# A new layout in SBUF for the split adjacency slices of a one-core GNN + LSTM kernel

## What is computed

```python
h = item_feat @ W_item.T + b_item            # 10000 x 128
b = layernorm(x) @ W_user.T + b_user
x = x + relu(adj @ h + b)                    # adj: 10000 x 10000, float32
xn = layernorm(x)[None]
hs = lstm(xn, W_ih, W_hh, b_ih, b_hh)
g  = argmax(hs @ W_lin.T + b_lin)            # gates what the two sums add up
w  = g * hs
x  = x + (2 * hs + (cumsum(w) - w) * fw_att + (total(w) - cumsum(w)) * bw_att)
```

## The kernel before

| slice, chunk | L882 (hi, item_hi) | L883 (lo, item_hi) | L884 (hi, item_lo) |
|---|---|---|---|
| 0, first | 64 | 192 | 256 |
| 0, second | 16 | 144 | 208 |
| 1, first | 480 | 96 | 160 |
| 1, second | 432 | 48 | 112 |
| 2, first | 384 | 0 | 64 |
| 2, second | 336 | 464 | 16 |
| 3, first | 288 | 416 | 480 |
| 3, second | 240 | 368 | 432 |

## Time and profile before

### The profile page before, as it was taken

How to read it: one execution, slowest core, us unless ns; L and a number is a source line. 1 busy time by engine, 2 the same in 40 slices (tenths; PEclk the granted TensorE clock), 3 DMA queues, 4 the chain that set the end, 5 groups by cost and what they waited for, 6 DMA issues and landing times.

```text
span 1427.8 us, 26195 instructions
## 1 busy us (share of the span) xinstructions
PE 1401.8 (98%) x7438; PEld 1210.5 (85%) x7438; DVE 1273.0 (89%) x2102; ACT 1056.4 (74%) x1449; POOL 213.4 (15%) x189
## 2 busy tenths in 40 slices
PE   8999999999999999999999999999999999999995
PEld 7888888888888888888888888888888899999995
DVE  7999999999999999999999999999999766676667
ACT  5677787777877877877877877877877676556663
POOL 0000000001001001001001001001000132036776
PEclk9999999999999999999999999999999999999998
DMA  9999999999999999999999999999999303000003
GB/s 373 344 336 382 399 387 392 394 385 383 405 385 395 391 387 397 392 382 402 384 387 402 391 377 405 387 380 402 388 388 382 133 1 144 0 2 0 0 0 145
DMA packets 143466, 442.96 MB, mean 310 GB/s; under 512 B 23944, under 2 KB 43337, under 8 KB 143307
## 3 DMA queue, kind: packets, MB, share of 16 engines
q1 hardware_dynamic: 126048, 426.43, 76.7%
q10 hardware_dynamic: 17387, 16.14, 4.0%
HBM read 432.15 MB, written 10.36 MB: 310 GB/s over the span
## 4 chain that ended last, share of the span: by engine, by line
PE 93%; DVE 5%; ACT 0%; issue 0%; DMA 0%; POOL 0%; ACTq 0%; DVEq 0%
PE psG L882 24%; PE psG L883 24%; PE psG L884 24%; PE psZ L980 10%; PE psZ L966 3%; PE psZ L968 3%; PE psZ L970 3%; DVE a_lo L1201 2%; PE psZ L986 1%; PE psT L857 1%; PE psI L930 1%; DVE item_lo L1234 1%; DVE u L1516 1%; DVE u L1215 0%; PE psG L875 0%
## 5 line engine op out<-in xcount | busy, mean ns | idle before, releaser
L665 ACT ACTIVATE a_hi<-raw 128x1000 fp32r<-128x1000 f32 (+1 forms) x800 | 819.5, 1030 | 241.9 <-PE psG L884 212.7
L1201 DVE TENSOR_TENSOR a_lo<-raw,a_hi 128x1000 fp32r<-128x1000 f32 (+1 forms) x800 | 897.8, 1171 | 22.9 <-ACT a_hi L665 19.9
L882 PE MATMUL psG<-a_hi,item_hi 128*128 128x500 f32 x1560 | 611.3, 392 | 2.3 <-DVE a_lo L1201 1.4
L883 PE MATMUL psG<-a_lo,item_hi 128*128 128x500 f32 x1560 | 606.0, 388 | 0.0
L884 PE MATMUL psG<-a_hi,item_lo 128*128 128x500 f32 x1560 | 604.6, 388 | 0.0
L882 PEld LDWEIGHTS psG<-a_hi,item_hi 128*128 128x128 f32 x1560 | 293.5, 188 | 65.5 <-DVE a_lo L1201 3.5
L884 PEld LDWEIGHTS psG<-a_hi,item_lo 128*128 128x128 f32 x1560 | 293.1, 188 | 59.5
L883 PEld LDWEIGHTS psG<-a_lo,item_hi 128*128 128x128 f32 x1560 | 293.7, 188 | 55.5
L980 PE MATMUL psZ<-hist,wh 128*128 (+1 forms) x1264 | 167.1, 275 | 2.9 <-DVE hist L1354 2.2
L980 PEld LDWEIGHTS psZ<-hist,wh 128*128 128x128 f32 x1264 | 154.0, 191 | 3.8 <-issue 2.4
L466 POOL TENSOR_TENSOR row_terms<-var,minus_half 125x4 f32<-125x4 f32 x20 | 37.6, 1878 | 677.9 <-DVE var L1152 677.9
(11 more groups left out here) (186 smaller groups left out, 857.1 us busy)
## 6 DMA issues: line engine op xcount, KB each, us to landing
raw<-in_adj_main SPq DMA_DIRECT2D x760, 500.0 KB, 6.6
raw<-in_adj_main SPq DMA_DIRECT2D x40, 250.0 KB, 4.7
sq<-rstd_copy ACTq DMA_DIRECT2D x20, 250.0 KB, 7.0
u<-x_copy SPq DMA_DIRECT2D x1, 5000.0 KB, 14.4
x_copy<-x_rows SPq DMA_DIRECT2D x19, 250.0 KB, 7.2
sq<-rows_copy ACTq DMA_DIRECT2D x19, 250.0 KB, 5.3
un_bb<-rows_copy ACTq DMA_DIRECT2D x19, 250.0 KB, 7.6
u<-in_itemT SPq DMA_DIRECT2D x9, 512.0 KB, 8.0
```

The source lines that it names most:

```text
L665: nc.scalar.activation(a_hi[:, s % CUT, 0:n], raw[:, r % RAW, at:at + n], ACT.Copy)\
L882: pe.matmul(bank, w_hi, hi, start=(c == 0), stop=False)
L883: pe.matmul(bank, w_hi, lo, start=False, stop=False)
L1201: last = dve.tensor_tensor(a_lo[:, s % CUT, 0:m], raw[:, r % RAW, at:at + m], a_hi[:, s % CUT, 0:m].bitcast(f32), ALU.subtract)
```

## The change

The two tensors `a_hi` and `a_lo` become one, `a_both`, in which places are worked out by numbers. The two chunks of a half piece begin 2048 bytes apart (`CHUNK = 512` elements) and not 2000, the slices 4048 bytes apart (`SLOT = 1012`) and not 4000. `item_tail` and `inv_rows` lose their own tensors and lie in columns of `x1_rows` that are not used yet at that time.

```diff
+CHUNK, SLOT = 512, 1012
+HI_AT, LO_AT, BOTH = 44, 4140, 8200
-        inv_rows = sb("inv_rows", [2, P])
-        item_tail = sb("item_tail", [P, STACKED], f32, first)
-        a_hi = sb("a_hi", [P, CUT, HALF * BW], f32r, first)
-        a_lo = sb("a_lo", [P, CUT, HALF * BW], f32r, first)
+        a_both = sb("a_both", [P, BOTH], f32r, first)
+        item_tail = x1_rows[:, 2 * HID:2 * HID + STACKED]
+        inv_rows = x1_rows[0:2, 3 * HID:4 * HID]
+        def chunk(at, s, i):
+            a = at + s % CUT * SLOT + i * CHUNK
+            return a_both[:, a:a + BW]
+        def chunks(at, s, n=HALF):
+            if n == 1:
+                return chunk(at, s, 0)
+            a = at + s % CUT * SLOT
+            return a_both[:, a:a + n * CHUNK].rearrange("p (c k) -> p c k", k=CHUNK)[:, :, 0:BW]
+        def by_chunk(t, n):
+            return t.rearrange("p (c k) -> p c k", k=BW) if n > BW else t
...
-                nc.scalar.activation(a_hi[:, s % CUT, 0:n], raw[:, r % RAW, at:at + n], ACT.Copy)\
+                nc.scalar.activation(chunks(HI_AT, s, n // BW), by_chunk(raw[:, r % RAW, at:at + n], n), ACT.Copy)\
...
-                            hi = a_hi[:, s % CUT, i * BW:(i + 1) * BW]
-                            lo = a_lo[:, s % CUT, i * BW:(i + 1) * BW]
+                            hi = chunk(HI_AT, s, i)
+                            lo = chunk(LO_AT, s, i)
...
-                last = dve.tensor_tensor(a_lo[:, s % CUT, 0:m], raw[:, r % RAW, at:at + m],
-                                         a_hi[:, s % CUT, 0:m].bitcast(f32), ALU.subtract)
+                last = dve.tensor_tensor(chunks(LO_AT, s, m // BW), by_chunk(raw[:, r % RAW, at:at + m], m),
+                                         chunks(HI_AT, s, m // BW).bitcast(f32), ALU.subtract)
```

More of the change, by code:

```diff
@@ L875, in body @@
                                 last = pe.matmul(bank, item_hi[0:STACKED, c * HID:(c + 1) * HID],
-                                                 a_hi[0:STACKED, s % CUT, i * BW:(i + 1) * BW], start=False, stop=True)
+                                                 chunk(HI_AT, s, i)[0:STACKED], start=False, stop=True)
                                 continue
-                            hi = a_hi[:, s % CUT, i * BW:(i + 1) * BW]
-                            lo = a_lo[:, s % CUT, i * BW:(i + 1) * BW]
+                            hi = chunk(HI_AT, s, i)
+                            lo = chunk(LO_AT, s, i)
                             w_hi = item_hi[:, c * HID:(c + 1) * HID]
@@ L1200, in split_lo @@
                 m = n - BW if tail else n
-                last = dve.tensor_tensor(a_lo[:, s % CUT, 0:m], raw[:, r % RAW, at:at + m],
-                                         a_hi[:, s % CUT, 0:m].bitcast(f32), ALU.subtract)
+                last = dve.tensor_tensor(chunks(LO_AT, s, m // BW), by_chunk(raw[:, r % RAW, at:at + m], m),
+                                         chunks(HI_AT, s, m // BW).bitcast(f32), ALU.subtract)
                 if tail:
                     mid = slice(STACK[1], STACK[1] + TAIL)
-                    last = dve.tensor_tensor(a_hi[mid, s % CUT, m:n], raw[mid, r % RAW, at + m:at + n],
-                                             a_hi[mid, s % CUT, m:n].bitcast(f32), ALU.subtract)
+                    short = chunk(HI_AT, s, 1)[mid]
+                    last = dve.tensor_tensor(short, raw[mid, r % RAW, at + m:at + n], short.bitcast(f32),
+                                             ALU.subtract)
                 last.then_inc(lo_ready, 1)
```

## The result

The changed kernel takes 1432.26 us (median of 11 executions), and the kernel before, on the same chips, 1427.95 us. The ratio is 1.0024, with a 95% interval of 1.0016 to 1.0033: 0.24% or 3.4 us slower (the two medians by themselves are 4.3 us apart). The forecast was 1425 us, 0.3% faster, with slower as a rival. The time is inside the range, the sign is wrong.

The account below looks back on a forecast made before the run. TensorE's matmul rate was taken as the bound. The four offsets' prices, 0.95 ns less on each of 4680 matmuls, gave -4.5 us from 1429.6, all other parts 0: 1425 us, range 1408 to 1439.

Parts of the forecast that it names:

- What bounds the kernel: TensorE, busy 98% of the span, sets the time of the 20 blocks; VectorE stands 2.6 us a block behind.
- Two runs of 500, `item_tail` and `inv_rows`, the LSTM at 0: Split ScalarE and VectorE accesses, moved first-block tensors, and the 303 us LSTM: each was to add 0 us.
- I price an offset with a matmul of before that has it to its own weights: TensorE's products: offsets 432, 384, 336, 288 priced at 383, 388, 389, 387 ns, mean 386.75; -4.5 us in all.
- The mean of before, taken as 387.7: Mean recorded duration of TensorE's 4680 matmuls before the change, 387.7 ns, against which the new offsets' 386.75 was set.
- The premise that a product lasts the same each time round the ring: TensorE's matmuls: the same slice and chunk gives the same duration each turn, with few exceptions; equal matmuls differ by 11 ns.
- 336 with 393 and 385 ns: One TensorE product at offset 336: 393 ns in the steady turn, 385 after a short stall; priced at the middle, 389.
- Rival B: One common offset lets TensorE's reads settle, most products near 383 ns: -22 us, 1408 us; chance 0.20.
- Rival C: Operand addresses modulo 512 do not cause TensorE's differing durations, so nothing changes: 1429.6 us; chance 0.15.
- Rival D: The weights loaded while a product streams matter: mean 390.75 ns, +14 us, 1444 us, half of that 1437; chance 0.25.

Follow-up runs that it names:

- the undo run: The changed kernel with slices back at the old offsets and `item_tail` its own tensor again, `a_both` and moved `inv_rows` kept: 1428.76 us, ratio 1.0003.
- the rings: TensorE alone playing the kernels' slice layouts, 144 distances each: before 225.6, changed 226.7, 16 bytes further 225.3, all slices at 448 220.0 ns.
- the map: TensorE alone, only matmuls, a run of 45 for each offset from 0 to 496, one start: 448 settled on 220.0 ns, 432 on 226.6.
- the pairs of the first map: TensorE alone, two weight tiles in turn at two distances to one moving chunk: 220.0 ns with both at 192 modulo 256; with 192 and 64, 220.0 or 228.

## Why the prediction was wrong

- **What bounds the kernel: right.** TensorE's distance from start to start set the time of both kernels (at 220 ns VectorE began to hold it back in places), and 0.9 ns on 4680 matmuls, 4.2 us, stands beside a measured 3.4 us by the ratio and 4.3 us by the medians.
- **Two runs of 500, `item_tail` and `inv_rows`, the LSTM at 0: right as far as shown.** VectorE's instruction took 1169 ns against 1171, and from the start of the last product to the end of the span there are 302.3 us in both profiles. With `inv_rows` moved the undo run had the time of before. `item_tail` was not tried alone, and TensorE reads both in the first block, which the prediction passes over; the rings leave no time for a cost of theirs. The price of the two runs was also less well founded than it reads: the runs of L1215 in the earlier trace rows lie without gaps.
- **"I price an offset with a matmul of before that has it to its own weights": this step failed.** It priced 432 at 383, 384 at 388, 336 at 389, 288 at 387 ns. Measured over blocks 2 to 20 they are 389.9, 388.8, 388.5 and 388.1, and the mean is 388.8 in place of 386.75. Of these 2.05 ns, 1.7 come from 432 alone. The mean of before, taken as 387.7, was right. The two products from which it was priced do stay short in the kernel before (382.7 and 383.8 ns in the mean), but in another sequence of offsets; in a run by itself on TensorE alone, and with all slices at 432, the offset gives 226.7 ns from start to start. The premise that a product lasts the same each time round the ring was also too strong: it holds within 1 ns for some nine in ten of the products of slices 1 to 3, and for six in ten of slice 0's first chunk. The row that could have warned me was in my own sum: 336 with 393 and 385 ns, for one product and one place. I took the middle of the two instead of asking what a value that depends on its predecessors says of a kernel with other predecessors.
- **Rival B, that a common offset helps:** the mechanism exists, since a run with one offset settles. But at half of the offsets in the map it settles on 226.7 ns, and at others on more or less. And the change keeps an offset for six products only, and none of its four (432, 384, 336, 288) stands at 220.0 in the map.
- **Rival C, that addresses are not the cause:** refuted, by the 18.7 us between 432 and 448. The Trainium skill, "SBUF — State Buffer", section "Who interferes with whom", says that TensorE's two read ports are independent. The traces disagree with what the prediction took from it, that the offset changes nothing: TensorE alone runs at 220.0 ns with 448 and at 226.7 ns with 432. That it is the ports that meet is not shown.
- **Rival D, the weights loaded meanwhile:** it named the right side, and its price (+14 us) was far too high. In the new layout the own and the next weights have one offset, so the kernels can't tell which of the two counts, nor can the pairs of the first map, and the upper value at each offset was no more a fixed price than mine.

What stays open is the mechanism inside, and so whether the own weights count or the next. All that the runs show is a step: each settled distance fits a short repeat of matmuls whose total is a multiple of 6.67 ns (220.0 and 226.7 for one, 446.7 for two at 223.3, 900.0 for four at 225.0, 686.7 for three at offset 32, where the 32 distances of the table average 228.8).

## What to carry to other kernels

Where TensorE is the bound and equal matmuls differ in the records, look at the start of the moving operand less that of the weights, modulo 256 bytes, and hold it at one good value through the kernel: here 16 or 192 gave 220.0 ns for 500 columns from all starts, most others some 226.7. Measure a repeating pattern as a pattern, with several starts, on the engine alone (here the rings of one such run gave the kernels' distances within 0.4 ns, where the map with one start misled at 400); a single instruction's duration read out of another rhythm is no price. And count the next engine's waits when the bound gets faster: one 1.07 us operation and its two split steps, placed one piece later in the block, were worth nothing before and 3.9 us after.

## What the runs showed of the hardware

- A 128x500 matmul with its own weight load takes 220.0 ns from start to start at best in a settled run at the 2.4 GHz level (granted clock 1.00), and 226.7 ns at half of the offsets in steps of 16 bytes, with no other engine at work.
- Settled runs of one offset are at 220.0 or 226.7 ns, 6.7 ns or 16 ticks of 2.4 GHz apart, or at 223.3, 225.0 and 228.8 in the mean. Offset 400 has both of the first two, by its start.
- The pattern repeats with 256 bytes (16 and 272, 192 and 448 alike), and a common shift of both operands by 64 to 448 bytes leaves the mean at 226.7 ns, tried at offsets 0 and 432.
